# First layer's attention: one weighing burst per group in place of two, and a ring of exponentials twice as deep

## The chip, the cores and the metric

One Trainium2 chip; the program runs on one of its cores. The metric is the device time in microseconds (us) of one execution. The engines are named as in the profile: PE (TensorE matmul), PEld (its weight load), DVE (VectorE), ACT (ScalarE), POOL (GpSimd) and SP (SyncE, which only issues DMAs here).

## The reference, cut to what matters

Four layers follow each other on an input of 8 sequences x 512 positions x 128 features; each is an attention times a gate from a feed-forward part. The change touches the attention of the first layer alone: 16 heads of 8 features, two query/key maps per head, causal, with a linear position bias.

```python
s0 = jnp.einsum('bhqd,bhkd->bhqk', q0, k0) * scale - bias + causal
s1 = jnp.einsum('bhqd,bhkd->bhqk', q1, k1) * scale - bias + causal
w0 = jax.nn.softmax(s0, axis=-1)
w1 = jax.nn.softmax(s1, axis=-1)
...
diff_weights = w0 - lamb * w1
heads = jnp.einsum('bhqk,bhkd->bhqd', diff_weights, v).transpose(0, 2, 1, 3)
```

## The kernel before, in words

`attend_phase` (L466) does this attention. Layer 0 calls it with two maps and masks (`causal` is true); layer 1 calls it with one map, without them, and takes the other branch of the constants. The 8 x 16 heads are worked in 64 groups of two heads; a group has four "units" x = 0 to 3 (two heads x two maps). The 512 positions are four blocks of 128.

For each group:

- **Pass 1** (`pass1`, L678 to L692, PE): scores with the queries on the partitions, in 11 cells. Cell 0 holds block 0 of all four units, cells 1 and 3 block 1 of two units each, and the others one block of one unit (2, 4, 6, 7: 384 columns; 5, 8, 9, 10: 512). Each cell goes to one bank of `pS`, which has SB = 4 banks used in turn. DVE takes its maxima over the keys (`extreme`, L818: L834 for the cells of several units, L826 for those of one), and that frees the bank.
- **The maxima**: PE transposes them (`turn_maxima`, L697), ACT negates them (L785), POOL splits them into three bf16 parts (`split`, L591), and SP writes these as three rows under the queries (`maxima`, L569).
- **Pass 2** (`pass2`, L699, PE): scores less the maxima with the keys on the partitions, in 10 cells, each one bank of `pX` (XB = 3 banks in turn). Cells 0 to 3 are key block 0 of the units, 4 to 7 key blocks 1 and 3, 8 and 9 key block 2 of two units. ACT takes the exponential into `E` (L779), and POOL cuts the diagonal blocks to the triangle (`cut`, L617).
- **Weighing** (`weigh`, L712, PE): per key block kt four f32 matmuls, one for each unit, on column tiles of the array, summed in the one bank `pO`. It waits for the cuts of the cells that hold kt. ACT copies `pO` out (`results`, L791), PE turns it (`turn_results`, L729), and DVE divides and stores (L848, L857, L859), POOL adds (L623).

The order is written out by hand. In `body` (L732) PE goes for group g through 10 slots s. In slot s it does pass 1 of the cells in `PLAN[s]` for group g + 2 (slot 0: cells 0 and 1; slot s: cell s + 1), with `turn_maxima(g + 1)` ahead of cell 2 and `turn_results(g - 1)` ahead of cell 7, then cell s + 1 of pass 2 (slot 9: cell 0 of group g + 1), and then the weighings that `WEIGHS` lists: kt 0 after slot 7 of its own group, and kt 1, 3, 2 after slot 2 of the next one (entry 12 = 10 + 2). ACT takes the exponentials in the order of pass 2, the negation after cell 1 and `results` after cell `RESULTS` = 3. DVE takes the cells in the order of pass 1. The two `pS` uses "tops" (transposed maxima) and "turned" (transposed results) are places 2 and 8 of the 13 in `SEQ`; they share the four banks with the cells. So a cell of pass 1 waits for the release of what stands four places ahead of it in `SEQ`: cell 3 for cell 0, cell 4 for cell 1, cell 5 for the tops, cell 10 for the turned results (`vacant`, L661).

`E` has NE = 10 places of 512 columns, one for each cell of pass 2, and ACT waits, for the cells that hold unit 0, until the group before has been weighed (L774 to L777).

Of the kernel before, what the change touches and what calls it, by code (L numbers as in the profile page):

```python
# [8 lines left out]
P = 128  # L9
# [7 lines left out]
ACT = mybir.ActivationFunctionType  # L17
# [256 lines left out]
class Arrivals:  # L274

    UN, NB = 4, 4
# [189 lines left out]
def attend_phase(nc, R, name, maps, arr, vtok, heads, lamb=None, negmax=None, aside=None):  # L466
# [6 lines left out]
    NB = 4  # L473
# [4 lines left out]
    DV = DH + 1  # L478
    q0 = lambda kt: kt * P if causal else 0
    if causal:  # L480
        CELLS = [((0, 1, 2, 3), 0), ((0, 1), 1), ((0,), 2), ((2, 3), 1), ((1,), 2), ((0,), 3), ((2,), 2), ((3,), 2), ((1,), 3), ((2,), 3), ((3,), 3)]
        PLAN = ((0, 1),) + tuple((c,) for c in range(2, 11))
        XCELLS = [((x, 0),) for x in range(UN)] + [((x, 1), (x, 3)) for x in range(UN)] + [((x, 2), (x + 1, 2)) for x in range(0, UN, 2)]
        ORDER = (0, 1, 3, 2)
        WEIGHS = {7: (0,), 12: (1, 3, 2)}
        SEQ = (0, 1, "tops", 2, 3, 4, 5, 6, "turned", 7, 8, 9, 10)
        RESULTS, STORES = 3, {0: (0,), 1: (1,)}
        SB, XB = 4, 3
        NE = len(XCELLS)
    else:  # L490
        CELLS = [((x, x), j) for x in range(UN) for j in range(0, QT, 2)]
        PLAN = tuple((s // 2,) if s % 2 == 0 else () for s in range(16))
        XCELLS = [((x, kt),) for kt in range(QT) for x in range(UN)]
        ORDER = (0, 1, 2, 3)
        WEIGHS = {4: (0,), 8: (1,), 12: (2,), 16: (3,)}
        SEQ = (0, "tops", 1, 2, 3, "turned", 4, 5, 6, 7)
        RESULTS, STORES = 2, {0: (0, 1)}
        SB, XB = 2, 3
        NE = 8
    NP1, NP2 = len(CELLS), len(XCELLS)  # L500
    cell_of = {xk: c for c, cell in enumerate(XCELLS) for xk in cell}
    ready = {kt: 1 + max(c for (x, k), c in cell_of.items() if k == kt) for kt in range(QT)}
    offset = {xk: sum(T - q0(k) for _, k in cell[:n]) for cell in XCELLS for n, xk in enumerate(cell)}
# [12 lines left out]
    BANK2, LAST2 = ring(NP2, XB)  # L516
    with phase(nc, name) as p:
# [4 lines left out]
        mp = p.sb("mp", [IT, 2, 3, P], BF16)  # L522
        E = p.sb("E", [P, NE, T])
        vs = p.sb("vs", [P, 2, GH, QT, DV])
        gs = p.sb("gs", [P, 2, GH])
# [4 lines left out]
        pX = p.ps("pX", [P, XB, T])  # L530
        pO = p.ps("pO", [P, T])
# [7 lines left out]
        s_e = p.sem("e")  # L539
# [16 lines left out]
        with nc.Block() as block:  # L556
# [28 lines left out]
            @block.gpsimd  # L585
            def _(pool):
                pool.wait_ge(arr.s_c, 16)
                nc.gpsimd.memset(vtok[:, :, :, DH:], 1.0)
                pool.drain()

                def split(at, h, early):  # L591

                    pool.wait_ge(s_m0, of(at, 1, h, 1))
                    if not early:
                        pool.wait_ge(s_mr[(h - 2) % NB], at(48, 48 * ((h - 2) // NB + 1)))
                    pool.nop(nofuse=True)
                    for k in range(3):
                        ins = nc.gpsimd.tensor_copy(mp[:, h % 2, k], m0[:, k])  # L598
                        if k < 2:
                            pool.drain()  # L600
                            nc.gpsimd.tensor_tensor(m0[:, k + 1], m0[:, k], mp[:, h % 2, k], ALU.subtract)
                            pool.drain()
                    ins.then_inc(s_mp, 1)

                def values(at, i, g, early):
                    if not early:
                        pool.wait_ge(s_pv, of(at, QT, g - 2, QT))
                    n = bass.ds((i * NB + g) * GH, GH)
                    nc.gpsimd.tensor_copy(gs[:, g % 2], gains[:, n])
                    nc.gpsimd.tensor_copy(vs[:, g % 2], vtok[:, n, :, :]).then_inc(s_vs, 1)  # L610

                def cut(at, g, c):
                    first, many = offset[XCELLS[c][0]], len(XCELLS[c])
                    own = E[:, c, :P] if many == 1 else E[:, c].rearrange("p (n w) -> p n w", w=P)[:, 0::offset[XCELLS[c][1]] // P]
                    pool.wait_ge(s_e, of(at, NP2, g, c + 1))
                    pool.nop(nofuse=True)
                    nc.gpsimd.affine_select(own, own, [[1, P]] if many == 1 else [[0, many], [1, P]], ALU.is_ge, 0.0, base=0, channel_multiplier=-1).then_inc(s_cut, 1)  # L617

                def joined(at, i, g):
                    dst = heads[:, bass.ds((i * NB + g) * GH * QT, GH * QT), :].rearrange("p (x j) d -> p x j d", j=QT)  # L620
                    pool.wait_ge(s_o1, of(at, 3, g, 3))
                    pool.nop(nofuse=True)
                    nc.gpsimd.tensor_tensor(dst, dst, o1[:, :, :, :], ALU.add).then_inc(s_st, 1)  # L623

                def body(i, first, last):
                    at = At(pool, i)
                    if first:
                        split(at, 0, True)
                        if causal:
                            values(at, i, 0, True)  # L630
                    for g in range(NB):
                        more = not (last and g + 1 >= NB)
                        if not causal:
                            values(at, i, g, first and g < 2)
                            if more:
                                split(at, g + 1, first and g + 1 < 2)
                            if aside is not None:
                                aside[0](pool, at, i, g, first)
                            continue
                        for c in range(NP2):  # L640
                            cut(at, g, c)
                            if c == 1 and more:
                                split(at, g + 1, first and g + 1 < 2)
                            if c == 6 and more:
                                values(at, i, g + 1, first and g + 1 < 2)
                            if c == 8 and not (first and g == 0):
                                joined(at, i, g - 1)

                    if last and causal:
                        joined(at, i, NB - 1)  # L650

                run_bodies(pool, COUNT, body)

            @block.tensor
            def _(pe):
# [56 lines left out]
                def weigh(at, g, kt, early):  # L712
                    if kt == 0:
                        pe.wait_ge(s_vs, of(at, 1, g, 1))
                        if not early:
                            pe.wait_ge(s_oT, of(at, 1, g, 0))
                    pe.wait_ge(s_cut if causal else s_e, of(at, NP2, g, ready[kt]))
                    w = T - q0(kt)
                    for x in range(UN):
                        o = offset[x, kt]  # L720
                        ins = nc.tensor.matmul(pO[32 * x:32 * x + DV, q0(kt):], vs[:, g % 2, x // maps, kt], E[:, cell_of[x, kt] % NE, o:o + w],  # L721
                                               start=(kt == ORDER[0]), stop=(kt == ORDER[-1]), tile_position=(0, 32 * x), skip_group_check=True)
                    ins.then_inc(s_pv, 1)

# [7 lines left out]
                def body(i, first, last):  # L732
# [9 lines left out]
                    for g in range(NB):  # L742
                        for s in range(NP2):
# [8 lines left out]
                            if not (last and h >= NB):  # L752
                                pass2(at, h, (s + 1) % NP2, first and h == 0)
                            for kt in WEIGHS.get(s + NP2, ()):
                                if not (first and g == 0):
                                    weigh(at, g - 1, kt, first and g == 1)
                            for kt in WEIGHS.get(s, ()):
                                weigh(at, g, kt, first and g == 0)
# [9 lines left out]
            def _(act):  # L768
                def expo(at, g, c, first):
                    x, kt = XCELLS[c][0]  # L770
                    if c == 0:
                        act.wait_ge(s_vs, of(at, 1, g, 1))
                    act.wait_ge(s_p2, of(at, NP2, g, c + 1))
                    if x == 0 and not (first and g == 0 and c < NE):  # L774
                        old = c - NE
                        held = max(ORDER.index(k) for _, k in XCELLS[old % NP2])
                        act.wait_ge(s_pv, of(at, QT, g, old // NP2 * QT + held + 1))  # L777
                    gain_of = x // maps
                    nc.scalar.activation(E[:, c % NE], pX[:, BANK2[(g * NP2 + c) % (NB * NP2)]], ACT.Exp, scale=gs[:, g % 2, gain_of:gain_of + 1]).then_inc(s_e, 1)  # L779

                def negate(at, h, early):
                    act.wait_ge(s_mt, of(at, 1, h, 1))
# [2894 lines left out]
```

## Time and profile before

| | us |
|---|---|
| time, median of 3 runs | 3793.6 |
| the three runs | 3791.26 to 3796.87 |
| the profiled execution | 3826.92 |
| its span, first to last instruction | 3825.1 |
| PE busy over the span | 3345.6 (87%) |
| DVE busy over the span | 2373.0 (62%) |
| ACT busy over the span | 2026.3 (53%) |
| attention of layer 0, first to last cut | 146.4 to 676.9 |

The profile's page gives shares over the whole program. The attention of layer 0 is about a seventh of it, and there the engines' shares differ from those of the page, so it is read with the views that take a stretch of time: the busy table, the list of waits, and above all the timeline. The profiled execution took 0.9% more than the median of the runs.

### The profile page before, as it was taken

Reading aid. Unit: us, or ns where it says so; the run is one execution under the profiler, and the core shown is the slowest. Engines: PE = TensorE matmul, PEld = TensorE weight load, DVE = VectorE, ACT = ScalarE, POOL = GpSimd, SP = SyncE. Lnnn points to the kernel's source line nnn. Section 1 sums busy time; section 2 is a strip of 40 time slices with the busy share of each in tenths; the row PEclk is TensorE's granted clock in tenths of the full one; section 3 lists DMA queues with packets and bytes.
Section 4 is the critical chain, followed back from the end, with each engine's and each line's share of the span. In section 5 each row is a group of like instructions: output and inputs, shape, how many; then the busy total and the mean of one; then the engine's idle time right before and its main releaser. Section 6 shows DMA issues by size and latency. Waiting matters only on the chain. (4 is left out here: it accounts for less than half of the span.)

```text
span 3825.1 us, 87256 instructions
## 1 busy us (share of the span) xinstructions
PE 3345.6 (87%) x26852; PEld 2091.7 (55%) x26852; DVE 2373.0 (62%) x6059; ACT 2026.3 (53%) x4169; POOL 1563.8 (41%) x2652
## 2 busy tenths in 40 slices
PE   4799999999967999859999867979874999999997
PEld 2344444777632222237777523679762666666664
DVE  5688887323346888667777755178356565666564
ACT  5588888443354888813333343333344666666662
POOL 0266667000011233227777626055571444444440
PEclk9799999999966999979999878878696999999999
DMA  5423322000022121145665211300033333333330
GB/s 135 105 70 76 74 72 63 22 6 12 4 74 63 48 47 44 26 93 156 162 159 158 77 64 37 104 6 3 13 59 73 102 117 117 117 117 117 117 97 23
DMA packets 200113, 289.70 MB, mean 76 GB/s; under 512 B 41100, under 2 KB 157004, under 8 KB 199520
## 3 DMA queue, kind: packets, MB, share of 16 engines
q1 hardware_dynamic: 195748, 277.81, 26.7%
q0 software_dynamic: 4096, 8.40, 1.4%
q8 instruction: 158, 2.59, 0.3%
q14 instruction: 111, 0.91, 0.1%
HBM read 234.81 MB, written 35.93 MB: 71 GB/s over the span
## 5 line engine op out<-in xcount | busy, mean ns | idle before, releaser
L779 ACT ACTIVATE att_E<-att_pX,att_gs 128x512 f32<-128x512 f32 x1152 | 718.0, 683 | 133.0 <-PE att_pX L708 132.3
L1957 POOL TENSOR_TENSOR att_E<-att_E,att_rz 128x128 f32<-128x128 f32 (+3 forms) x512 | 357.4, 719 | 436.1 <-DVE att_rz L2167 436.1
L834 DVE TENSOR_REDUCE att_mx<-att_pS 128x2 f32<-128x1024 f32 (+2 forms) x448 | 434.7, 992 | 86.7 <-PE att_pS L686 71.9
L686 PE MATMUL att_pS<-arr_ks,arr_qs 72*128 72x512 bf16 (+4 forms) x1536 | 423.0, 339 | 50.7 <-DVE att_mx L834 27.6
L708 PE MATMUL att_pX<-arr_qs,arr_ks 75*128 75x512 bf16 (+4 forms) x1536 | 420.8, 329 | 8.9 <-DMA arr_qs<-att_mp 4.8
L1697 POOL TENSOR_TENSOR pairs_h<-pairs_m,pairs_r 128x512 f32<-128x512 f32 x272 | 345.6, 1271 | 194.0 <-DVE pairs_m L1760 129.1
L1721 PEld LDWEIGHTS pairs_po<-pairs_a,pairs_h 128*128 128x128 f32 x2176 | 286.5, 192 | 130.4 <-issue 129.2
L826 DVE CUSTOM_DVE_ANT_0 att_seen<-att_pS,arr_later 128x384 bf16<-128x384 f32 (+1 forms) x512 | 298.8, 613 | 80.4 <-PE att_pS L686 80.0
L1742 ACT ACTIVATE pairs_r<-pairs_ph 128x512 f32<-128x512 f32 x272 | 162.4, 597 | 330.1 <-PE pairs_ph L1713 328.9
L721 PE MATMUL att_pO<-att_E,att_vs 128*9 128x512 f32 (+3 forms) x3072 | 298.5, 491 | 9.2 <-ACT att_E L779 8.7
L2099 ACT ACTIVATE att_E<-att_S,att_nm 128x128 f32<-128x128 f32 (+3 forms) x512 | 283.0, 557 | 40.3 <-DVE att_nm L2161 40.1
L2161 DVE CUSTOM_DVE_ANT_0 att_S<-att_pS,att_bias 128x128 f32<-128x128 f32 (+3 forms) x512 | 229.3, 484 | 104.0 <-PE att_pS L1998 99.0
L1713 PE MATMUL pairs_ph<-xnT,pairs_a 128*128 128x512 f32 x544 | 282.9, 603 | 11.6 <-DMA pairs_a<-in_down_dram 11.6
L1721 PE MATMUL pairs_po<-pairs_a,pairs_h 128*128 128x128 f32 x2176 | 287.5, 275 | 0.3 <-POOL pairs_h L1697 0.3
L617 POOL TENSOR_SCALAR_AFFINE_SELECT att_E<-att_E 128x256 f32<-128x256 f32 (+1 forms) x640 | 227.3, 359 | 138.6 <-ACT att_E L779 133.0
L1760 DVE SCALAR_TENSOR_TENSOR pairs_m<-pairs_ph,pairs_c 128x512 f32<-128x512 f32 x272 | 188.2, 692 | 142.9 <-ACT pairs_r L1742 134.5
L686 PEld LDWEIGHTS att_pS<-arr_ks,arr_qs 76*128 76x128 bf16 (+1 forms) x1536 | 134.0, 99 | 258.8 <-DVE att_mx L834 100.4
L708 PEld LDWEIGHTS att_pX<-arr_qs,arr_ks 127*128 127x128 bf16 (+1 forms) x1536 | 149.3, 98 | 219.6 <-ACT att_E L779 123.9
L1225 PEld LDWEIGHTS ex_po<-ex_a,ex_h 128*128 128x128 f32 x1536 | 201.3, 192 | 91.2 <-issue 88.0
L1283 ACT ACTIVATE ex_h<-ex_ph,ex_bs 128x512 f32<-128x512 f32 x192 | 131.3, 686 | 183.7 <-PE ex_ph L1216 183.7
L598 POOL CAST att_mp<-att_m 16x128 bf16<-16x128 f32 x288 | 80.5, 280 | 311.8 <-ACT att_m L785 286.6
L2008 PE MATMUL att_pT<-ident,att_E 128*128 128x128 f32 x1280 | 194.3, 274 | 10.1 <-DVE att_WT L2175 2.1
(413 smaller groups left out, 6458.9 us busy)
## 6 DMA issues: line engine op xcount, KB each, us to landing
pairs_c<-weights SPq DMA_DIRECT2D x272, 256.0 KB, 3.9
att_bias<-in_bias_dram SPq DMA_DIRECT2D x64, 896.0 KB, 5.1
parts<-proj_part SPq DMA_DIRECT2D x144, 128.0 KB, 2.3
att_xb<-xnT SPq DMA_DIRECT2D x64, 256.0 KB, 5.4
arr_qs<-parts SPq DMA_DIRECT2D x192, 64.0 KB
arr_ks<-parts SPq DMA_DIRECT2D x192, 64.0 KB
att_w<-in_w3a_dram SPq DMA_DIRECT2D x64, 192.0 KB, 5.1
arr_qs<-parts SPq DMA_DIRECT2D x96, 96.0 KB
```

The costliest lines, as they stand in the source:

```text
L686: ins = nc.tensor.matmul(pS[:, bank, n * w:(n + 1) * w], qs[:K1, u, x, q * P:(q + 1) * P], ks[:K1, u, x, :w], start=(n == 0 or not causal) ...
L708: ins = nc.tensor.matmul(pX[:, bank, o:o + w], ks[:, g % NB, x, kt * P:(kt + 1) * P], qs[:, g % NB, x, q0(kt):], start=(n == 0), stop=True ...
L721: ins = nc.tensor.matmul(pO[32 * x:32 * x + DV, q0(kt):], vs[:, g % 2, x // maps, kt], E[:, cell_of[x, kt] % NE, o:o + w], start=(kt == OR ...
L779: nc.scalar.activation(E[:, c % NE], pX[:, BANK2[(g * NP2 + c) % (NB * NP2)]], ACT.Exp, scale=gs[:, g % 2, gain_of:gain_of + 1]).then_inc( ...
L826: V.tensor_tensor_reduce(out=seen[:, own, :w], in0=pS[:, bank, :w], in1=arr.later[:, T - w:], scale=1.0, scalar=-3.0e38, op0=ALU.add, op1= ...
L834: V.reduce_max(dst, src, AX.X).then_inc(s_mx, 1)
L1697: nc.gpsimd.tensor_tensor(h[:, g % RING], m[:, g % RING], r[:, g % RING], ALU.mult).then_inc(s_h, 1)
L1713: nc.tensor.matmul(ph[:, g % RING], a[:, v, 0], R.xnT[:, b * T:(b + 1) * T], start=True, stop=True).then_inc(s_up, 1)
L1721: ins = nc.tensor.matmul(po[:, g % RING, q * P:(q + 1) * P], h[:, g % RING, q * P:(q + 1) * P], a[:, v, 1], start=True, stop=True)
L1957: nc.gpsimd.tensor_tensor(E[:, k, :width(j)], E[:, k, :width(j)], rz[:, u, k:k + 1].broadcast_to([P, width(j)]), ALU.mult).then_inc(s_n, 1)
L2099: nc.scalar.activation(E[:, k, :width(j)], S[:, r % RING, :width(j)], ACT.Exp, bias=nm[:, u, k:k + 1], scale=-1.0, accum_out=Z[:, u, k:k + ...
L2161: nc.vector.tensor_tensor_reduce(out=S[:, r % RING, :w_], in0=pS[:, r // 2 % 2, h, :w_], in1=bias[:, u, off:off + w_], scale=-1.0 / DW, sc ...
```

## The change

`WEIGHS` is now `{13: (0, 1, 3, 2)}`: nothing is weighed in a group's own slots; all four key blocks are weighed in one burst after slot 3 of the next group. `RESULTS` goes from 3 to 4. `NE` goes from 10 to 20, and the writers and readers of `E` (exponential, cut, weighing) take place (10 g + c) mod 20, since a group's exponentials now live on beside those of the next group. The work is the same.

```diff
-        WEIGHS = {7: (0,), 12: (1, 3, 2)}
+        WEIGHS = {13: (0, 1, 3, 2)}
         SEQ = (0, 1, "tops", 2, 3, 4, 5, 6, "turned", 7, 8, 9, 10)
-        RESULTS, STORES = 3, {0: (0,), 1: (1,)}
+        RESULTS, STORES = 4, {0: (0,), 1: (1,)}
         SB, XB = 4, 3
-        NE = len(XCELLS)
+        NE = 2 * len(XCELLS)
...
+                    place = (g * NP2 + c) % NE
+                    own = E[:, place, :P] if many == 1 else E[:, place].rearrange("p (n w) -> p n w", w=P)[:, 0::offset[XCELLS[c][1]] // P]
...
-                    if x == 0 and not (first and g == 0 and c < NE):
+                    if x == 0 and not (first and g * NP2 + c < NE):
...
-                    nc.scalar.activation(E[:, c % NE], pX[:, BANK2[(g * NP2 + c) % (NB * NP2)]], ACT.Exp, scale=gs[:, g % 2, gain_of:gain_of + 1]).then_inc(s_e, 1)
+                    nc.scalar.activation(E[:, (g * NP2 + c) % NE], pX[:, BANK2[(g * NP2 + c) % (NB * NP2)]], ACT.Exp, scale=gs[:, g % 2, gain_of:gain_of + 1]).then_inc(s_e, 1)
```

The weighing's matmul reads `E[:, (g * NP2 + cell_of[x, kt]) % NE, o:o + w]` in the same way. In layer 1 NE stays 8 and a group has 16 cells, so that every index and wait there is what it was.

## Rows read from the trace of the kernel before

**Rows 1.** Busy table: stretch, busy us of each engine (instructions), granted clock, DMA share, GB/s.
```profile
300.00:600.00 300.00, 299.77 (x2639) 144.25 (x2641) 253.38 (x847) 247.88 (x442) 208.86 (x661) 1.00 0.31 74
```

**Rows 2.** Timeline of PE, one group: start us, us, what, shape, count.
```profile
406.99 1.05 PE L721 MATMUL att_pO<-att_E,att_vs 128*9 128x512 f32 x8
407.97 0.39 PE L686 MATMUL att_pS<-arr_ks,arr_qs 76*128 76x512 bf16 x1
...
408.64 0.38 PE L708 MATMUL att_pX<-arr_qs,arr_ks 127*128 127x512 bf16 x1
...
409.98 0.27 PE L697 MATMUL att_pS<-ident,att_mx 128*16 128x128 f32 x1
...
410.51 0.39 PE L686 MATMUL att_pS<-arr_ks,arr_qs 76*128 76x256 bf16 x2
...
410.85 0.38 PE L708 MATMUL att_pX<-arr_qs,arr_ks 127*128 127x512 bf16 x1
411.16 1.48 PE L721 MATMUL att_pO<-att_E,att_vs 128*9 128x384 f32 x24
412.58 0.34 PE L686 MATMUL att_pS<-arr_ks,arr_qs 76*128 76x384 bf16 x1
412.75 0.39 PE L708 MATMUL att_pX<-arr_qs,arr_ks 127*128 127x384 bf16 x2
412.97 0.38 PE L686 MATMUL att_pS<-arr_ks,arr_qs 76*128 76x512 bf16 x1
...
415.15 1.05 PE L721 MATMUL att_pO<-att_E,att_vs 128*9 128x512 f32 x8
```

**Rows 3.** Timeline of DVE, one group; in brackets its idle time before, and the releaser.
```profile
404.93 0.56 DVE L826 CUSTOM_DVE_ANT_0 att_seen<-att_pS,arr_later 128x384 bf16<-128x384 f32 x1 [0.97 <-PE att_pS L686]
...
405.41 0.69 DVE L826 CUSTOM_DVE_ANT_0 att_seen<-att_pS,arr_later 128x512 bf16<-128x512 f32 x1
...
406.50 0.26 DVE L848 RECIPROCAL att_rz<-att_pS 128x16 f32<-128x16 f32 x1
...
407.54 0.68 DVE L826 CUSTOM_DVE_ANT_0 att_seen<-att_pS,arr_later 128x512 bf16<-128x512 f32 x1
408.15 0.08 DVE L826 DVE_READ_ACCUMULATOR2_ANT att_mx<- 128x1 f32 x1
408.54 0.69 DVE L826 CUSTOM_DVE_ANT_0 att_seen<-att_pS,arr_later 128x512 bf16<-128x512 f32 x1 [0.31 <-PE att_pS L686]
...
409.77 1.28 DVE L834 TENSOR_REDUCE att_mx<-att_pS 128x4 f32<-128x512 f32 x2
410.97 0.55 DVE L826 CUSTOM_DVE_ANT_0 att_seen<-att_pS,arr_later 128x384 bf16<-128x384 f32 x1
```

**Rows 4.** Waits, 300 to 600 us: us in total, times, longest.
```profile
DVE att_seen L826 <- PE att_pS L686: 46.6, 73, 1.0
...
PEld att_pS L686 <- DVE att_mx L834: 27.2, 73, 0.4
...
PEld att_pO L721 <- issue: 23.8, 111, 0.3
```

**Rows 5.** Timeline of ACT, the same group.
```profile
404.55 0.60 ACT L791 ACTIVATE att_oT<-att_pO 128x512 f32<-128x512 f32 x1 [0.69 <-PE att_pO L721]
...
410.63 0.25 ACT L785 ACTIVATE att_m<-att_pS 16x128 f32<-16x128 f32 x1
```

**Rows 6.** SP's issues of the maxima, and their time from issue to landing.
```profile
413.37 1.78 SPq L569 DMA_DIRECT2D arr_qs<-att_mp  x3
...
DMA to landing us min/median/max: 1.6/1.9/3.2
```

**Rows 7.** Timeline of PE: first burst, the last beside pass 1, the last group's.
```profile
158.42 1.05 PE L721 MATMUL att_pO<-att_E,att_vs 128*9 128x512 f32 x8
...
660.46 1.05 PE L721 MATMUL att_pO<-att_E,att_vs 128*9 128x512 f32 x8
...
674.71 1.05 PE L721 MATMUL att_pO<-att_E,att_vs 128*9 128x512 f32 x8
```

More of the change, by code:

```diff
@@ L613, in cut @@
                     first, many = offset[XCELLS[c][0]], len(XCELLS[c])
-                    own = E[:, c, :P] if many == 1 else E[:, c].rearrange("p (n w) -> p n w", w=P)[:, 0::offset[XCELLS[c][1]] // P]
+                    place = (g * NP2 + c) % NE
+                    own = E[:, place, :P] if many == 1 else E[:, place].rearrange("p (n w) -> p n w", w=P)[:, 0::offset[XCELLS[c][1]] // P]
                     pool.wait_ge(s_e, of(at, NP2, g, c + 1))
@@ L720, in weigh @@
                         o = offset[x, kt]
-                        ins = nc.tensor.matmul(pO[32 * x:32 * x + DV, q0(kt):], vs[:, g % 2, x // maps, kt], E[:, cell_of[x, kt] % NE, o:o + w],
+                        ins = nc.tensor.matmul(pO[32 * x:32 * x + DV, q0(kt):], vs[:, g % 2, x // maps, kt], E[:, (g * NP2 + cell_of[x, kt]) % NE, o:o + w],
                                                start=(kt == ORDER[0]), stop=(kt == ORDER[-1]), tile_position=(0, 32 * x), skip_group_check=True)
```

## Prediction

> **What bounds it now.** I read the busy table of the stage first: from 300 to 600 us PE is busy for 299.77 of 300.00 us, DVE for 253.38 and ACT for 247.88, at a granted clock of 1.00 [rows 1]. That looks like a stage bound by PE alone, with 15% to spare on DVE. But PE's busy time is a union of overlapping records and hides short waits, so the list of waits comes next. It shows two sides at once: DVE waits for pass 1 46.6 us in 73 waits, two per group, and PE waits for DVE's reduction (L834) 27.2 us, also in 73 waits, and starts its bursts after gaps that nothing releases (23.8 us in 111) [rows 4]. So each engine is late for the other at some point of the group. The timeline says where. A group takes 415.15 - 406.99 = 8.16 us [rows 2]. PE has two weighing bursts: kt 0 from 406.99 to the next matmul at 407.97 (0.98), and kt 1, 3, 2 from 411.16 to 412.58 (1.42) [rows 2]. During each, PE makes no cell of pass 1, and DVE runs dry just behind each: idle 0.97 ahead of cell 4 and 0.31 ahead of cell 9 [rows 3]. DVE has no slack that it can use at will: 6.88 us of work plus these two holes (1.28) are the 8.16.
>
> **What the change does on PE.** The matmuls are the same. A burst costs an entry and an exit besides its columns. Entry: from the last cell of pass 2 to the burst 411.16 - 410.85 = 0.31, where two matmul cells stand 412.97 - 412.75 = 0.22 apart, so 0.09. Exit: kt 0 has 512 columns and took 0.98; kt 1, 3, 2 have 384 + 128 + 256 = 768 and took 1.42; 256 columns make 0.44, so 512 make 0.88, and 0.10 is left as a fixed part [rows 2]. (0.98 and 1.42 add up to 2.40; one burst of 1280 columns is 2.40 - 0.10 = 2.30; if the fixed part is 0.13, it is 2.27. I take 2.28.) PE's own sum per group falls by 0.09 + 0.12 = 0.21 us. If PE alone set the pace, that would be 61 x 0.21 = 13 us gained.
>
> At the entry and exit the row shows 0.09 and 0.10 to 0.13 us around a burst. The Trainium skill, "TensorEngine Tiling (Array Packing)", Key Properties, says that a change of the tiling mode (here whole array to column tiles) drains TensorE; by that rule, and the trace agrees with it, one pair of drains goes away in each group and the stage gets faster. It is the rule that speaks for the first rival below.
>
> **What the merged burst does to DVE.** The banks of pS decide. When PE enters the burst (now after slot 3), its last cell of pass 1 is cell 4, and cell 4 may only be written when DVE has released cell 1. Hence at most cells 2, 3 and 4 are left for DVE while PE weighs. I follow the loop from DVE's start on cell 1 (time 0), with every step from a row:
> - cell 1 is a reduction (L834); release to PE: cell 0's started at 409.77, and cell 3, which needs that bank, started at 410.51: 0.74 [rows 2, 3].
> - PE: cell 4 and its cell of pass 2, 412.58 to 412.97: 0.39; entry 0.09; burst 2.28 [rows 2]. PE writes cell 5 at 0.74 + 0.39 + 0.09 + 2.28 = 3.50.
> - DVE starts a 512-column cell 0.57 after PE does (407.97 to 408.54) [rows 2, 3]: cell 5 starts on DVE at 4.07.
> - DVE by then has done cells 1 to 4: two reductions take 410.97 - 409.77 = 1.20, so 0.60 each, and a 384-column cell 405.41 - 404.93 = 0.48 [rows 3]: 0.60 + 0.48 + 0.60 + 0.48 = 2.16. It stands idle for 4.07 - 2.16 = 1.91 us.
> - From cell 5 to the next group's cell 1, DVE has its work back to back: cell 5 to the start of cell 8, divide and store among it, 407.54 - 405.41 = 2.13; cell 8, 408.15 - 407.54 = 0.61; cells 9 and 10, 409.77 - 408.54 = 1.23; cell 0, 0.60; in all 4.57 [rows 3].
>
> The period is 4.07 + 4.57 = **8.64 us**. The same loop for before, as a test of the method: from cell 0's reduction at 409.77 PE reaches cell 3 at 410.51, the burst at 411.16, cell 4 at 412.58, and DVE starts cell 4 at 404.93 + 8.16 = 413.09: 3.32 in all; from there to the next reduction of cell 0, 409.77 - 404.93 = 4.84; in all 8.16 [rows 2, 3]. The two idle times 0.97 and 0.31 become one of about 1.9: split bursts let DVE live on its three queued cells twice, a merged one only once.
>
> **What else moves, and what hides it.** (a) `results` now comes after cell 4 of ACT. ACT starts it 0.13 us behind the first matmul after the burst (404.55 + 8.16 = 412.71 against 412.58) and takes 0.60, so PE can turn the results from about 0.75 on [rows 2, 5]. PE itself reaches that point after cells 5 and 6, some 0.8 behind the burst, and DVE asks for the turned results 1.09 after it starts cell 5 (405.41 to 406.50) [rows 3], which is 1.66 behind the burst. Level or a little to spare: priced 0 to 0.05. (b) The maxima. Now the transpose stands 409.98 - 408.64 = 1.34 behind cell 0 of pass 2, the negation 410.63 - 408.64 = 1.99 behind it, SP's issues begin at 413.37, the third some 1.2 later, and it lands 1.9 after that, at about 416.45, 7.8 behind cell 0; the next cell 0 comes 8.16 behind the last [rows 2, 5, 6]. In the new order the transpose still waits for DVE's cell 10, 0.83 behind its start (409.15, which is 408.54 + 0.61, to 409.98) [rows 2, 3]: 0.57 + 2.13 + 0.61 + 0.61 + 0.83 = 4.75 behind the burst. PE is at cell 0 of pass 2 after 416.80 (408.64 + 8.16) - 412.97 = 3.83 less the burst that went (0.98 + 0.09), 2.76, or some 0.3 more if cell 10 waits for the bank of the turned results, which DVE leaves only just ahead of cell 8 (0.57 + 2.13 = 2.70). So the transpose stands 1.7 to 2.0 behind cell 0, the negation 2.1 to 2.6, the landing 7.9 to 8.4, and the next cell 0 at 8.64: it hides, with 0.2 to 0.7 us to spare, and is priced 0. The ten loads for g + 3 that stand ahead of it on SP start with the end of pass 2 as now, and are no later against it. (c) The exponentials no longer wait for the weighing of the group before (20 places). Nobody waits for that now in a way the list shows, so 0. (d) POOL's cuts: all ten of a group are done long before slot 3 of the next, so the burst never waits for them.
>
> **Sum.** +0.48 per group. The bursts of groups 0 to 60 fall into groups that still have pass 1; first to last burst beside pass 1, 158.42 to 660.46, are 61 periods of 8.23 on average [rows 7]. 61 x 0.48 = +29. Off that: 502.04 - 61 x 8.16 = 4.3 us are stalls above the steady pace in the early groups; a longer period hides part: -3. The last two groups have no pass 1 (660.46 to 674.71, 7.1 each [rows 7]); ACT sets their pace, and the merged burst holds it by at least 0 and at most 0.98 each, plus a last burst that is longer by kt 0: together 0 to 2.8, I take +1, since the three pX banks cover part as the pS banks do. In all +27: the profiled execution would go from 3826.9 to about 3854, and the median of the runs, 0.9% lower, from 3793.6 to 3820. Bounds: burst 2.27 to 2.30, DVE's response 0.51 (384-column case) to 0.57, (a) up to 0.05, and the period's sum +0.42 to +0.56: 26 to 34; with the early stalls fully absorbed and the tail at its ends, 21 to 37.
>
> **Rivals.**
> 1. *Faster: PE alone sets the pace.* If DVE could take more than three cells during the burst, the entry and exit saved would be all that is seen: 61 x 0.21 = -13 us, 3781. For it: PE's busy share [rows 1]. Against it: DVE is already dry behind both bursts [rows 3], and 27.2 us of PE's time are waits for the reduction that frees the bank [rows 4]. It decides if DVE's idle time in a group stays at or below 1.28 - 0.21 = 1.07 us. Chance 0.06.
> 2. *No change:* the saved entry and the longer hole cancel, as when PE gets further ahead before the burst than I have it. DVE's idle would stay near 1.28 per group: 3794, within 8 us. Chance 0.06.
> 3. *Half of it, +9 to +19 us:* the hole is about 1.6, if cell 4 is released earlier than the loop says. About 3808. Chance 0.13.
> 4. *Slower still: the maxima arrive late.* If the negation slips by more than the slack of 0.2 to 0.7 us in (b), cell 0 of pass 2 waits for the DMA in every group. With landings up to 3.2 [rows 6] the price is 0.1 to 0.9 us per group on top, +33 to +80 in all; about 3845. Chance 0.10.
> 5. *The forecast*, DVE starved by the merged burst, 3813 to 3832: chance 0.65.
>
> The Trainium skill's "Perfetto Trace Analysis", Optimization Strategy, says that a gap that repeats on the engine that should be saturated can mean too few buffers; the repeating gap here is PE's 0.3 to 0.4 us ahead of cells that wait for DVE [rows 4], and the change adds places to E, which nobody waits for, and none to pS.
>
> **How the numbers follow.** The likeliest case gives 3820. The range takes the forecast, rival 3 and the lower part of rival 4: 3803 to 3838. About 0.2% (8 us) is what a measurement of this kernel can tell from no change. Faster by more than that: 0.06. Within it: 0.08 (rival 2 and the low end of rival 3). Slower: 0.86.
>
> **What would show it.** DVE's timeline should have one hole per group, 1.8 to 1.9 us, ahead of cell 5 (the first 512-column cell), and none ahead of cell 9; groups 8.6 us apart; one burst of about 2.3 us per group; PE waiting for L834 ahead of cell 4 and for DVE's L826 about 0.5 us ahead of the transpose of the maxima; PE's busy share of the stage below 97%. I am wrong if groups are 7.9 to 8.2 us apart, if DVE's hole is below 1.3 us, or if waits for the maxima's DMA appear in most groups.

## The result: 1% slower, and where DVE stands idle

The changed kernel takes 3830.8 us (median of 4 runs, 3825.0 to 3834.9) against 3792.4 us before (3791.2 to 3796.9): +38 us, ratio 1.0098, 95% interval 1.0080 to 1.0116. A second comparison, made later, in which the kernel before takes 3819.6 us, gives 3851.7, +32 us, ratio 1.0082 (1.0067 to 1.0096).

The profiled execution of the changed kernel (3824.97 us) is no longer than that of before (3826.92). The stage itself tells why that is no contradiction: from the first to the last cut it takes 711.1 - 147.6 = 563.5 us against 676.9 - 146.4 = 530.5 before, +33 us. The rest of the program, which the change does not touch, was 35 us shorter in the one execution than in the other (3259.2 against 3294.6 us). Spans of two profiled executions could not have been subtracted here; the stage's own length could. That 33 us is also all that the profiles explain: what made the first comparison +38 and not +33 is open.

The busy table of the changed kernel has lost PE's full house (columns as in [rows 1]):

```profile
300.00:600.00 300.00, 284.82 (x2460) 140.86 (x2459) 236.78 (x789) 235.22 (x411) 194.58 (x617) 1.00 0.27 69
```

PE is busy for 284.82 of 300 us, DVE for 236.78 and ACT for 235.22: all three do less per us. The timeline of PE shows one group from burst to burst (the counterpart of [rows 2]; line numbers are one higher than before; the rows at 405.62 and 405.84 are cell 10 of pass 1 and cell 0 of pass 2):

```profile
400.27 2.34 PE L722 MATMUL att_pO<-att_E,att_vs 128*9 128x512 f32 x32
402.55 0.39 PE L687 MATMUL att_pS<-arr_ks,arr_qs 76*128 76x512 bf16 x1
...
403.16 0.38 PE L709 MATMUL att_pX<-arr_qs,arr_ks 127*128 127x384 bf16 x2
403.49 0.65 PE L730 MATMUL att_pS<-ident,att_oT 128*128 128x128 f32 x4
403.98 0.33 PE L687 MATMUL att_pS<-arr_ks,arr_qs 76*128 76x384 bf16 x1
...
405.62 0.39 PE L687 MATMUL att_pS<-arr_ks,arr_qs 76*128 76x512 bf16 x1 [0.21 <-DVE heads L860]
405.84 0.38 PE L709 MATMUL att_pX<-arr_qs,arr_ks 127*128 127x512 bf16 x1
...
406.84 0.38 PE L709 MATMUL att_pX<-arr_qs,arr_ks 127*128 127x512 bf16 x1
407.52 0.27 PE L698 MATMUL att_pS<-ident,att_mx 128*16 128x128 f32 x1 [0.30 <-DVE att_mx L827]
...
408.65 0.34 PE L687 MATMUL att_pS<-arr_ks,arr_qs 76*128 76x384 bf16 x1
...
409.13 2.34 PE L722 MATMUL att_pO<-att_E,att_vs 128*9 128x512 f32 x32
411.41 0.39 PE L687 MATMUL att_pS<-arr_ks,arr_qs 76*128 76x512 bf16 x1
```

The burst takes 402.55 - 400.27 = 2.28 us, as forecast, and one entry and exit are gone. But the group takes 409.13 - 400.27 = 8.86 us. (It is the longest of a pattern of four, 8.72, 8.72, 8.86 and 8.80; before, the four are 8.16, 8.16, 8.17 and 8.22.) The transpose of the maxima (407.52) now waits for DVE: 0.68 us behind the cell of pass 2 ahead of it, of which the cell takes 0.22. DVE's timeline shows the cause (the counterpart of [rows 3]):

```profile
400.12 0.69 DVE L835 TENSOR_REDUCE att_mx<-att_pS 128x2 f32<-128x512 f32 x1
400.72 0.55 DVE L827 CUSTOM_DVE_ANT_0 att_seen<-att_pS,arr_later 128x384 bf16<-128x384 f32 x1
...
403.17 0.69 DVE L827 CUSTOM_DVE_ANT_0 att_seen<-att_pS,arr_later 128x512 bf16<-128x512 f32 x1 [1.90 <-PE att_pS L687]
...
403.79 0.55 DVE L827 CUSTOM_DVE_ANT_0 att_seen<-att_pS,arr_later 128x384 bf16<-128x384 f32 x1
...
404.27 0.26 DVE L849 RECIPROCAL att_rz<-att_pS 128x16 f32<-128x16 f32 x1
404.54 0.56 DVE L827 CUSTOM_DVE_ANT_0 att_seen<-att_pS,arr_later 128x384 bf16<-128x384 f32 x1
...
405.47 0.68 DVE L827 CUSTOM_DVE_ANT_0 att_seen<-att_pS,arr_later 128x512 bf16<-128x512 f32 x1
...
407.30 1.29 DVE L835 TENSOR_REDUCE att_mx<-att_pS 128x4 f32<-128x512 f32 x2
...
411.97 0.69 DVE L827 CUSTOM_DVE_ANT_0 att_seen<-att_pS,arr_later 128x512 bf16<-128x512 f32 x1 [1.84 <-PE att_pS L687]
```

Where [rows 3] had two holes, 0.97 and 0.31, there is one of 1.84 to 1.90 us, ahead of cell 5. After it DVE works with hardly a break until cell 4 of the next group. The list of waits from 300 to 600 us (as [rows 4]) sums it up:

```profile
DVE att_seen L827 <- PE att_pS L687: 62.9, 34, 1.9
ACT att_oT L792 <- PE att_pO L722: 50.4, 34, 1.5
...
PEld att_pS L698 <- DVE att_mx L827: 20.3, 34, 0.7
```

There are 34 waits of DVE in place of 73, one per group, of 1.85 us on average. No wait for the maxima's DMA is in the list.

### The profile page after: what moved, and what is told of

Same layout as the page of the kernel before. It is cut to its first block and busy times, and to the rows that moved or that the text cites. A ratio compares the mean times of both kernels' runs of the same rounds, so it can differ in the third digit from the quotient of the medians.

```text
span 3822.7 us, 87282 instructions
## 1 busy us (share of the span) xinstructions
PE 3332.0 (87%) x26852; PEld 2091.4 (55%) x26852; DVE 2373.8 (62%) x6059; ACT 2032.9 (53%) x4169; POOL 1569.2 (41%) x2652
## 5 line engine op out<-in xcount | busy, mean ns | idle before, releaser
L780 ACT ACTIVATE att_E<-att_pX,att_gs 128x512 f32<-128x512 f32 x1152 | 720.8, 683 | 106.4 <-PE att_pX L709 99.1
L722 PE MATMUL att_pO<-att_E,att_vs 128*9 128x512 f32 (+3 forms) x3072 | 284.6, 488 | 8.6 <-ACT att_E L780 8.4
```

The costliest lines, as they stand in the source:

```text
L780: nc.scalar.activation(E[:, (g * NP2 + c) % NE], pX[:, BANK2[(g * NP2 + c) % (NB * NP2)]], ACT.Exp, scale=gs[:, g % 2, gain_of:gain_of + 1 ...
```

## The experiments

The measure for all of them is the time per group: the distance between the first and the last transpose of the maxima that start between 300 and 600 us, divided by the groups between them. Before, these are at 303.68 and 598.08: 294.40 / 36 = 8.178 us. In the changed kernel they are at 302.22 and 591.82: 289.60 / 33 = 8.776. The second profiles of the same two kernels give 8.189 and 8.773, so a few hundredths can be told apart. All kernels here repeat in fours, the length of a loop body, so a single group can lie some tenths off its mean. The ratios are against runs of the kernel before beside them on the same chip.

| kernel | us per group | ratio of times (95% interval) |
|---|---|---|
| before, once more | 8.189 | 1.0005 (0.9995 to 1.0016) |
| the change, once more | 8.773 | 1.0082 (1.0067 to 1.0096) |
| ring of 20 places alone | 8.184 | 1.0000 (0.9989 to 1.0010) |
| two bursts, the later after slot 3 | 8.336 | 1.0018 (1.0008 to 1.0028) |
| one burst after slot 2 | 8.639 | 1.0074 (1.0057 to 1.0091) |
| the change, results turned a cell later | 8.647 | 1.0077 (1.0060 to 1.0094) |
| one burst after slot 4, turned later | 8.792 | 1.0094 (1.0080 to 1.0109) |
| before, short maxima | 8.038 | 0.9985 (0.9975 to 0.9995) |
| the change, short maxima | 8.085 | 0.9981 (0.9971 to 0.9992) |
| the change, short kt 0 | 8.135 | 0.9994 (0.9982 to 1.0005) |
| before, kt 0 after slot 8 | 8.117 | 0.9985 (0.9976 to 0.9994) |
| before, kt 0 after slot 9 | 8.855 | 1.0119 (1.0104 to 1.0134) |

**The two kernels once more.**

> The kernel before once more, for a second profile: its first profiled execution had the stage at 530 us but all the rest 35 us longer than the profile of the changed kernel. If that was only the execution, the stage is again 530 us (8.17 us per group) and the rest is near 3260 us.

> The changed kernel once more, beside its relatives on one chip: 8.78 us per group, 61 x 0.60 - 4 + 1 = +33 us, ratio 1.009.

Measured: the time per group as above, 3820.2 us for before. Its stage takes 529.0 us, as expected, but the rest is 3287.5 us and not near 3260: that expectation failed. In thirteen of the fourteen profiles of this case the rest is 3286 to 3295 us; the changed kernel's first profile, with 3259, is the one that stands apart. In the second profile of the changed kernel the rest is 3293.4 and the stage 562.9 us. The difference of the pair is 8.773 - 8.189 = 0.58 us per group, and for 61 groups 36 us, against 32 us in the times.

**Which part of the change costs.** First the ring alone, the two bursts as before:

```diff
-        WEIGHS = {13: (0, 1, 3, 2)}
+        WEIGHS = {7: (0,), 12: (1, 3, 2)}
-        RESULTS, STORES = 4, {0: (0,), 1: (1,)}
+        RESULTS, STORES = 3, {0: (0,), 1: (1,)}
```

> Only the ring of exponentials doubled, the two bursts as before. Theory (DVE is starved by the merged burst): 8.17 us per group and the time of the kernel before within 0.2%. Rival (the wider ring itself costs, by its addresses or its register sums): part of the +0.60 us per group shows here.

8.184 us per group, ratio 1.0000. The twenty places cost and bring nothing by themselves. Then the later place without the merging:

```diff
-        WEIGHS = {13: (0, 1, 3, 2)}
+        WEIGHS = {7: (0,), 13: (1, 3, 2)}
```

> The changed kernel with kt 0 back after slot 7: two bursts, the later one after slot 3 as in the change. Theory: the hole ahead of cell 5 is 0.74 + 0.39 + 0.09 + 1.42 + 0.57 - 2.16 = 1.05 us and a small one stays ahead of cell 9, so 8.2 to 8.3 us per group, 3792 to 3800. Rival (the later place or the results after cell 4 is what costs, not the merging): near 8.78 us per group, 3829.

8.336 us: 0.16 above before, 0.44 below the change, and a little above the 8.2 to 8.3 expected. The ratio 1.0018 makes +7 us, the upper end of what was expected. DVE's holes in this kernel (timeline of DVE):

```profile
399.94 0.69 DVE L827 CUSTOM_DVE_ANT_0 att_seen<-att_pS,arr_later 128x512 bf16<-128x512 f32 x1 [0.98 <-PE att_pS L687]
...
403.26 0.69 DVE L827 CUSTOM_DVE_ANT_0 att_seen<-att_pS,arr_later 128x512 bf16<-128x512 f32 x1 [0.34 <-PE att_pS L687]
```

0.98 and 0.34, nearly as before. So three quarters of the loss belong to the merging; the rest comes with the place after slot 3. Its timeline of PE shows where: the turning of the results (L730) stands 400.31 - 399.99 = 0.32 us behind the cell ahead of it and takes 0.49 to the next cell, where the kernel before has 0.22 and 0.44.

```profile
399.99 0.38 PE L709 MATMUL att_pX<-arr_qs,arr_ks 127*128 127x384 bf16 x2
400.31 0.65 PE L730 MATMUL att_pS<-ident,att_oT 128*128 128x128 f32 x4
400.80 0.33 PE L687 MATMUL att_pS<-arr_ks,arr_qs 76*128 76x384 bf16 x1
```

The mirror test merges at the old place:

```diff
-        WEIGHS = {13: (0, 1, 3, 2)}
+        WEIGHS = {12: (0, 1, 3, 2)}
-        RESULTS, STORES = 4, {0: (0,), 1: (1,)}
+        RESULTS, STORES = 3, {0: (0,), 1: (1,)}
```

> One burst of all four key blocks, but after slot 2, with the results after cell 3 as before. Theory: the same hole of 1.9 us, since cells 1, 2 and 3 are as much work for DVE as 2, 3 and 4, and the turning of the results has a slot more of room, which takes away the 0.14 us that the changed kernel lost there: 8.63 us per group, 3820. Rival (place, not merging): close to 8.2.

8.639 us per group against 8.63 expected, ratio 1.0074, +28 us. DVE's hole is the same size, ahead of cell 4:

```profile
400.26 0.56 DVE L827 CUSTOM_DVE_ANT_0 att_seen<-att_pS,arr_later 128x384 bf16<-128x384 f32 x1 [1.88 <-PE att_pS L687]
```

**The 0.13 us that the forecast did not have.** If the results are turned one cell later, PE has another slot before it needs them:

```diff
-        SEQ = (0, 1, "tops", 2, 3, 4, 5, 6, "turned", 7, 8, 9, 10)
+        SEQ = (0, 1, "tops", 2, 3, 4, 5, 6, 7, "turned", 8, 9, 10)
```

> The changed kernel with the results turned one cell later (ahead of cell 8 in place of cell 7). Theory: PE has a slot more before it needs the copied results, DVE no longer finds cell 7 late, and the group falls from 8.78 to 8.64 us, the time by 8 us to about 3822. If the loss of 0.14 us per group lies elsewhere, it stays at 8.78.

8.647 us, 0.13 less than the change: the loss was there. The stage is 557.2 us, 6 us shorter than in the change. The times do not tell the two apart: +27 us here and +32 for the change, each against its own runs of before, and the intervals overlap, so the 8 us that were expected of the time are not shown by it. In this kernel DVE goes through cells 5, 6, 7 and the reciprocals without a break, and the hole is the old one:

```profile
406.62 0.69 DVE L827 CUSTOM_DVE_ANT_0 att_seen<-att_pS,arr_later 128x512 bf16<-128x512 f32 x1 [1.83 <-PE att_pS L687]
...
407.23 0.55 DVE L827 CUSTOM_DVE_ANT_0 att_seen<-att_pS,arr_later 128x384 bf16<-128x384 f32 x1
...
407.71 0.55 DVE L827 CUSTOM_DVE_ANT_0 att_seen<-att_pS,arr_later 128x384 bf16<-128x384 f32 x1
...
408.19 0.26 DVE L849 RECIPROCAL att_rz<-att_pS 128x16 f32<-128x16 f32 x1
408.36 0.63 DVE L827 CUSTOM_DVE_ANT_0 att_seen<-att_pS,arr_later 128x512 bf16<-128x512 f32 x1
```

**Is it DVE?** The strongest rival to "DVE is starved" was that something else reacts to the merged burst: ACT waits 1.5 us for it too, the maxima might land late, the burst might be dearer. Making DVE's work light tells these apart, since it leaves the burst, ACT and the maxima's way as they are. Both kernels got the same edit:

```diff
-                        V.tensor_tensor_reduce(out=seen[:, own, :w], in0=pS[:, bank, :w], in1=arr.later[:, T - w:], scale=1.0, scalar=-3.0e38,
+                        V.tensor_tensor_reduce(out=seen[:, own, :P], in0=pS[:, bank, w - P:w], in1=arr.later[:, T - P:], scale=1.0, scalar=-3.0e38,
```

> The kernel before with DVE's maxima taken over only the last 128 keys of each single cell (part of the maxima left out; eight of its eleven maxima per group cost a fraction). Theory: PE loses only its short waits for DVE, 8.17 to about 7.97 us per group.

> The changed kernel with the same shortened maxima. Theory (DVE starved): the cost of the merged burst is gone, and with one entry and exit less it needs 0 to 0.21 us per group less than its partner, 7.76 to 7.97. Rival (ACT starved by the burst, or the maxima landing late, or a dearer burst): it still stands 0.4 us or more per group above its partner.

8.038 and 8.085 us per group; 3814.4 and 3814.8 us. Both are above what was expected (7.97, and 7.76 to 7.97). But the gap of 0.6 us is gone to 0.05, although the hole of DVE has grown to 2.41 us (the row below, from the changed kernel with short maxima) and the burst is as long:

```profile
403.63 0.29 DVE L827 CUSTOM_DVE_ANT_0 att_seen<-att_pS,arr_later 128x128 bf16<-128x128 f32 x1 [2.41 <-PE att_pS L687]
```

A hole costs nothing when DVE has time to spare; it was DVE's rate over the rest of the group that turned it into time. The pair also says how near PE's own pace lay before the change: with DVE light the group falls only from 8.18 to 8.04. The saved entry and exit (0.21) hardly show even here. Two neighbouring bursts of PE's timeline are 7.95 us apart, where the partner has 7.99, but the four groups of the pattern take 7.97, 7.95, 8.36 and 8.04 us, where the partner's take 7.98, 7.99, 8.17 and 7.99:

```profile
400.79 2.34 PE L722 MATMUL att_pO<-att_E,att_vs 128*9 128x512 f32 x32
403.06 0.39 PE L687 MATMUL att_pS<-arr_ks,arr_qs 76*128 76x512 bf16 x1
...
408.74 2.34 PE L722 MATMUL att_pO<-att_E,att_vs 128*9 128x512 f32 x32
```

What eats it is partly to be seen. The turning of the results stands 0.25 to 0.33 us behind the cell ahead of it and takes 0.49 to the next one, against 0.22 and 0.44 in the partner. In the group of 8.36, cell 9 of pass 2 also comes 0.28 us late, and the list of waits has such a wait for ACT's exponentials (L780) once in four groups. The rest was not taken apart.

**The size of the burst.** Less weighing, same structure:

```diff
-                        ins = nc.tensor.matmul(pO[32 * x:32 * x + DV, q0(kt):], vs[:, g % 2, x // maps, kt], E[:, (g * NP2 + cell_of[x, kt]) % NE, o:o + w],
-                                               start=(kt == ORDER[0]), stop=(kt == ORDER[-1]), tile_position=(0, 32 * x), skip_group_check=True)
+                        last = P if causal and kt == 0 else T
+                        ins = nc.tensor.matmul(pO[32 * x:32 * x + DV, q0(kt):last], vs[:, g % 2, x // maps, kt], E[:, (g * NP2 + cell_of[x, kt]) % NE, o:o + last - q0(kt)],
+                                               start=(kt in (0, 1) if causal else kt == 0), stop=(kt == ORDER[-1]), tile_position=(0, 32 * x), skip_group_check=True)
```

> The changed kernel with the weighing of key block 0 cut to its first 128 of 512 query columns (the rest of that block's contribution is left out): the burst is 0.66 us shorter (2.28 to 1.62). Theory: the hole shrinks one for one, 8.78 to about 8.12 us per group. Rival (a fixed cost of the merged burst, or the maxima's chain sets the pace): less than half of the 0.66 comes off.

The timelines of PE and DVE:

```profile
403.78 0.27 PE L698 MATMUL att_pS<-ident,att_mx 128*16 128x128 f32 x1 [0.30 <-DVE att_mx L828]
```

```profile
407.59 0.69 DVE L828 CUSTOM_DVE_ANT_0 att_seen<-att_pS,arr_later 128x512 bf16<-128x512 f32 x1 [1.20 <-PE att_pS L687]
```

The next transpose is at 411.86, 8.08 us later; the mean of all groups is 8.135, where about 8.12 was expected. The holes are 1.20 to 1.26, against 1.84 to 1.90, that is 0.64 less for a burst 0.64 shorter (1.64 from 405.39 to 407.03), and the group is 8.776 - 8.135 = 0.64 shorter. Over this step it is one for one. The time, ratio 0.9994, is that of before. (The output is not right here, since part of the weighing is left out.)

**How much work lies in the banks.** The loop says that the hole depends on how many cells DVE has in hand when the burst begins. After slot 4 it has one more:

```diff
-        WEIGHS = {13: (0, 1, 3, 2)}
-        SEQ = (0, 1, "tops", 2, 3, 4, 5, 6, "turned", 7, 8, 9, 10)
-        RESULTS, STORES = 4, {0: (0,), 1: (1,)}
+        WEIGHS = {14: (0, 1, 3, 2)}
+        SEQ = (0, 1, "tops", 2, 3, 4, 5, 6, 7, "turned", 8, 9, 10)
+        RESULTS, STORES = 5, {0: (0,), 1: (1,)}
```

> One burst of all four key blocks after slot 4, results after cell 5 of ACT, turned ahead of cell 8. Theory (what counts is how much work for DVE lies in the banks of pS when the burst begins): cells 2 to 5 lie there, since the tops' bank is freed by ACT and cell 5 doesn't wait for DVE. From DVE's start on cell 1 to cell 6: 0.74 + 0.39 + 0.44 + 0.09 + 2.28 + 0.51 = 4.45, less 2.77 of work = a hole of 1.68; 4.45 + 3.96 = 8.41 us per group, ratio about 1.004. Rival (any merged burst costs the same): 8.64 or more.

Half of that held. The hole is 1.61 to 1.67, as expected (1.68), but the group takes 8.792 us, no less than the change, and the expectation of 8.41 failed. The rows show where the rest went:

```profile
402.74 0.56 DVE L827 CUSTOM_DVE_ANT_0 att_seen<-att_pS,arr_later 128x384 bf16<-128x384 f32 x1 [1.67 <-PE att_pS L687]
...
403.22 0.55 DVE L827 CUSTOM_DVE_ANT_0 att_seen<-att_pS,arr_later 128x384 bf16<-128x384 f32 x1
...
403.79 0.26 DVE L849 RECIPROCAL att_rz<-att_pS 128x16 f32<-128x16 f32 x1
404.21 0.69 DVE L827 CUSTOM_DVE_ANT_0 att_seen<-att_pS,arr_later 128x512 bf16<-128x512 f32 x1 [0.15 <-issue]
```

From cell 6 to cell 8 DVE takes 404.21 - 402.74 = 1.47 us where its work is 0.48 + 0.48 + 0.17 = 1.13: the turned results are once more too close behind the burst, and DVE waits for them and for cell 8. These 0.34 are most of the 0.38 us by which the group is longer than the 8.41 expected. By the group's time alone the rival, any merged burst costs the same, cannot be told from this; only the hole speaks against it. Moving a burst to where the banks are fuller moves its other neighbours as well.

**A version that would beat both?** If DVE's holes are the price, the small burst of the kernel before might stand better one cell later, and the maxima's loop might forbid two cells later (`{9: (0,), 12: (1, 3, 2)}`):

```diff
-        WEIGHS = {7: (0,), 12: (1, 3, 2)}
+        WEIGHS = {8: (0,), 12: (1, 3, 2)}
```

> The kernel before with kt 0 weighed after slot 8 in place of slot 7, still two bursts and ten places. Theory: cell 9 reaches DVE before the small burst, 0.98 us earlier, so the hole of 0.31 ahead of cell 9 becomes one of about 0.2 ahead of cell 10, DVE is some 0.15 earlier with the maxima, PE's wait for them at the transpose goes, and a group takes 8.0 to 8.05 us: 7 to 10 us less, ratio 0.9975 to 0.998. Rival (the stage is PE's, DVE's holes are idle time): no change.

> The same with kt 0 after slot 9, thus between cell 0 of pass 2 and the transpose of the next maxima. Theory (loop of the maxima): the transpose, the negation and the landing fall 0.85 to 0.98 us later behind cell 0 of pass 2, 7.8 + 0.85 = 8.65 us, so waits for the maxima's DMA appear in most groups and set a period of about 8.6 to 8.7. If that loop has more room than read, 8.0 to 8.2.

After slot 8: 8.117 us per group, ratio 0.9985 (0.9976 to 0.9994), the medians 4 us less than before and the ratio 6, where 7 to 10 were expected. It is the fastest kernel here that computes everything, by an amount at the edge of what can be measured. Three groups of four take 7.98 to 8.04 us, as expected or better; every fourth takes 8.45. In that one PE waits for ACT ahead of cell 9 of pass 2 (timeline of PE):

```profile
409.41 0.38 PE L686 MATMUL att_pS<-arr_ks,arr_qs 76*128 76x512 bf16 x1
410.08 0.39 PE L708 MATMUL att_pX<-arr_qs,arr_ks 127*128 127x256 bf16 x2 [0.29 <-ACT att_E L779]
```

The kernel's `ring` gives the last of the 40 cells in a body the pX bank used two cells earlier instead of three. Before, the burst of kt 0 stood just ahead of that cell, and its list has no such wait; here it stands behind it. No run changed this ring, so that it explains the 8.45 is not shown. After slot 9: 8.855, ratio 1.0119, a little more than expected. But that run doesn't isolate the maxima's loop, as it was meant to. Its list of waits names another wait that I had not reckoned with:

```profile
ACT att_E L779 <- PE att_pO L721: 39.7, 34, 1.2
```

With ten places, ACT's cell 0 of the next group may only overwrite kt 0's exponentials when they have been weighed, and after slot 9 that is too late. The maxima's DMA waits as well (0.31 us ahead of cell 0 of pass 2 in its timeline), but behind that. Which of the two sets the 8.86 was left open.

## Why the prediction was right, and which term was too small

**Direction and mechanism: right.** The loop through the four banks of pS gave 4.07 us from DVE's start on cell 1 to its start on cell 5. The changed kernel has 407.30 + 0.60 = 407.90 to 411.97: 4.07. The burst was put at 2.28 and is 2.28. DVE's idle time was put at 1.91 and is recorded as 1.84 to 1.90. (The profile's brackets begin about 0.08 later than the sum's count, which follows starts: from the start on cell 1, 2.16 of work to 411.97 leaves 1.91 here too. By the same token the old holes are 1.28 in brackets but 1.44 in that count, which is why the hole seems to grow by more than the period.) The light-DVE pair, the one-for-one answer to a shorter burst and the same hole after slot 2 show that this loop set the pace; the delay of the turned results adds to its second half. No run gave pS more banks, which would be the direct test.

**Size: +27 us forecast, +38 and +32 measured.** The term that was too small is (a), the turned results, priced at 0 to 0.05 us per group; it measured 0.13. The second half of the loop, cell 5 to the next cell 1, was put at 4.57 and is 411.97 less 403.17 less 4.07 = 4.73. The excess lies between cells 5 and 8: 405.47 - 403.17 = 2.30 in place of 2.13. PE turns the results 403.49 - 403.16 = 0.33 us behind the cell ahead of them where 0.22 is the rule, and so cell 7, which stands behind the turning on PE, reaches DVE late: DVE's reciprocals end their turn and cell 7 starts at 404.54, 0.27 behind the reciprocals' start in place of 0.17, and takes 0.48 in place of 0.42. I had compared the time at which the results are ready with the time at which DVE wants them, and not with cell 7, which queues behind them on PE. `turn_later` takes the whole of it away, and `one_burst_slot2` never has it: 8.647 and 8.639, against 8.64 in the forecast. That it agrees to 0.01 is partly luck, since single groups of these kernels take 8.62 to 8.70. With it the sum is 61 x (8.776 - 8.178) = 36, less the early stalls that are absorbed, plus 1 for the tail, about 33: the stage's growth from first to last cut.

The groups that are written out, ahead of the loop and behind it, have the forecast's value: between the first four bursts there are 8.65, 8.65 and 8.66 us, behind the loop 8.65 (681.07 to 689.72), and in the loop 8.72 to 8.86. Two things differ. First, the results' copy on ACT starts 0.13 us behind PE's first matmul after the burst in the written-out groups (first two rows, changed kernel), but 0.21 in the first two of each four groups in the loop (third row, where PE's matmul is at 402.55), and 0.13 or 0.14 in the other two.

```profile
174.62 0.39 PE L687 MATMUL att_pS<-arr_ks,arr_qs 76*128 76x512 bf16 x1
```

```profile
174.75 0.60 ACT L792 ACTIVATE att_oT<-att_pO 128x512 f32<-128x512 f32 x1 [1.47 <-PE att_pO L722]
```

```profile
402.76 0.60 ACT L792 ACTIVATE att_oT<-att_pO 128x512 f32<-128x512 f32 x1 [1.44 <-PE att_pO L722]
```

The kernel before has the same two values in its loop, 0.21 in the first two of each four groups and 0.13 or 0.14 in the other two; [rows 5] is one of the latter, and this is one of the former:

```profile
420.74 0.34 PE L686 MATMUL att_pS<-arr_ks,arr_qs 76*128 76x384 bf16 x1
```

```profile
420.95 0.60 ACT L791 ACTIVATE att_oT<-att_pO 128x512 f32<-128x512 f32 x1 [0.77 <-PE att_pO L721]
```

There it did not reach the turning, which stood 0.22 behind the cell ahead of it in all groups: PE came to it a slot later. So the price of 0 to 0.05 rested on the better half of the groups. Second, even the looped groups of the changed kernel whose copy starts at 0.14 are longer than the written-out ones: the turning starts 0.24 to 0.25 us behind the cell ahead and takes 0.49, against 0.22 and 0.44, and the group takes 8.72 against 8.65. With the copy at 0.21 the turning starts 0.33 behind, and the group takes 8.80, or 8.86 where the hole is 1.90 and not 1.84. No run was made that would show why the copy and the turning are later in the loop.

**Tail: right in size.** From the last burst that pass 1 follows at once to the next two there are 7.82 and 7.43 us (689.72, 697.54, 704.97), against 7.55 and 7.02 between the bursts of kt 1, 3, 2 before (656.46, 664.01, 671.03), and from there to the last cut 6.10 against 5.91: +0.9 together, where +1 was taken.

**Early stalls.** Of the 4.3 us above the steady pace before, the forecast let 3 be hidden. The 4.3 were counted against 8.16, the pace of three groups in four; against the mean of 8.178 they are 3.2. The stage grew by 33 us where 36 + 1 would be the full sum, so 3 to 4 were absorbed, part of it by the written-out groups with their 8.65.

**Rivals.** PE's own pace (-13 us) is out: PE's busy share fell, and even with DVE light the two kernels are level. (The 27.2 us of [rows 4] that the prediction counted as PE's time are waits of PEld, the weight load, which overlap PE's matmuls. In [rows 2] cell 3 starts only 410.51 - 410.26 = 0.25 behind the cell ahead of it, where 0.22 is the rule.) Late maxima are out for the change: no such wait in the list. Their slack did shrink as worked out in (b): the transpose stands 407.52 - 405.84 = 1.68 us behind cell 0 of pass 2, 1.34 before, and 1.7 to 2.0 forecast. The bank of the turned results holds cell 10 up by 0.21 us, where 0.3 was allowed for. One bound of (b) was wrong in itself: a negation 0.65 behind the transpose gives 2.3 to 2.6 behind cell 0, not 2.1 to 2.6, and a slack of 0.2 to 0.5, not 0.7. Nothing rested on it, since ACT negated at 407.84, 2.00 behind cell 0.

**On the drain between tilings.** The rows agreed that an entry and an exit cost about 0.2 us, and one pair did go. It was worth nothing here, where the loop through DVE is the longer one, and did not show with DVE light either.

## What to carry to other kernels

PE was 99.9% busy, and yet its work alone did not set the pace: look for a producer and a consumer that wait for each other at different places of the same period, and follow one loop through the buffers between them. Merging stretches in which a producer gives nothing saves its switching cost once, but the consumer lives through it on one set of buffers in place of two; count the work that lies in them when the stretch begins. When a step is moved towards what depends on it, compare not only when its result is ready and wanted, but what else queues behind it.

## What was not expected of the hardware

The same instruction (ACT's copy of pO) started 0.13 us after PE went on in the groups that are written out, but 0.21 us in the first two of each four looped groups and 0.13 or 0.14 in the other two, in the kernel before as in the changed one. The time per group in the loop follows a pattern of four in both (8.16, 8.16, 8.17, 8.22 us before; 8.72, 8.72, 8.86, 8.80 us after). Its cause is open. And the rest of the program, untouched by the change, took 3286 to 3295 us in thirteen profiled executions and 3259 in one, a difference as large as the effect itself.
